# Sinkhorn steps of the stream mixer placed behind the key stages alone

## What is computed

```python
# layer 1: linear cross attention, q from layernorm(x), k and v from the context
qh = softmax(Wq q, over the 64 rows of a head) / 8
kh = softmax(Wk k, over the 2048 columns)
context = einsum('bhdn,bhen->bhde', kh, Wv v)
x = x + rmsnorm_over_channels(Wo (context applied to qh) + bo) * g * 16
# layer 2: four streams of 512 columns per token (a token is a row of 2048)
H_res = sinkhorn_log(logits_res, num_iters=50, tau=0.1)   # 4 x 4 per token
H_pre, H_post = softmax(logits_pre), softmax(logits_post)
y = einsum('btjc,btj->btc', x_streams, H_pre) @ W_branch
x = x + ((1-g) I + g H_res) mixed over the streams + y * H_post
```

## Time and profile before

| | |
|---|---|
| median of 3 runs | 2906.38 us (2905.24 to 2907.76) |
| the profiled execution | 2906.39 us, its span 2904.7 us |
| mean granted TensorE clock | 0.967 |
| TensorE busy | 2626.9 us (90%) |
| VectorE busy | 1663.3 us (57%) |
| ScalarE busy | 1033.0 us (36%) |
| GpSimd busy | 804.3 us (28%) |

### The profile page before, as it was taken

The page is one execution under the profiler, slowest core; times in us unless marked ns, Lnnn a source line. Parts: engine busy times, 40 slices in busy tenths (PEclk is TensorE's granted clock), DMA queues, the critical chain, the costliest instruction groups (busy, mean ns, idle before and its releaser), DMA issues.

```text
span 2904.7 us, 32933 instructions
## 1 busy us (share of the span) xinstructions
PE 2626.9 (90%) x11002; PEld 1735.8 (60%) x11002; DVE 1663.3 (57%) x4194; ACT 1033.0 (36%) x2312; POOL 804.3 (28%) x785
## 2 busy tenths in 40 slices
PE   7989898999989898999989999898998999999765
PEld 4766666666656566565666656566665566656411
DVE  2444434345766757355664766534587685867482
ACT  2333333334332333434333343333434333343222
POOL 1322314050422304142231513214051141512311
PEclk9999999999999999999999999999999999999878
DMA  6112121203112120413324221232413324231166
GB/s 223 37 55 91 58 95 54 92 22 107 39 55 91 59 95 29 140 61 105 120 76 128 70 89 64 82 121 67 137 61 104 122 71 133 69 100 32 52 180 169
DMA packets 203082, 258.22 MB, mean 89 GB/s; under 512 B 45218, under 2 KB 111522, under 8 KB 202914
## 3 DMA queue, kind: packets, MB, share of 16 engines
q1 hardware_dynamic: 202914, 256.12, 28.0%
HBM read 180.17 MB, written 75.89 MB: 88 GB/s over the span
## 4 chain that ended last, share of the span: by engine, by line
PE 77%; DVE 14%; ACT 3%; issue 2%; DMA 1%; POOL 1%; SPq 1%; DVEq 0%; ACTq 0%; POOLq 0%
PE big L628 16%; PE kc_bank L571 15%; PE big L546 13%; PE big L603 13%; PE tb L670 4%; PE tb L613 4%; PE tb L557 4%; PE misc L650 3%; PE tb L681 3%; DVE stats L800 2%; ACT turned L1138 2%; PE kc_bank L647 2%; DVE ska L974 1%; DVE skr L977 1%; DMA out<-mix_out 1%
## 5 line engine op out<-in xcount | busy, mean ns | idle before, releaser
L1138 ACT COPY turned<-tb 128x512 f32<-128x512 f32 x512 | 297.8, 585 | 1021.1 <-PE tb L613 692.7
L546 PE MATMUL big<-ctx_sb,wk 128*128 128x512 f32 x1024 | 515.2, 632 | 50.3 <-ACT k_exp L1129 50.1
L628 PE MATMUL big<-merged,turned 128*128 128x256 f32 x2048 | 492.9, 383 | 61.7 <-ACT turned L1138 61.1
L628 PEld LDWEIGHTS big<-merged,turned 128*128 128x128 f32 x2048 | 380.5, 190 | 206.5 <-issue 123.6
L571 PE MATMUL kc_bank<-ctxt,turned 128*128 128x256 f32 x2048 | 481.8, 379 | 6.8 <-ACT turned L1138 6.8
L603 PE MATMUL big<-wqs,x_sb 128*128 128x512 f32 x1024 | 482.0, 596 | 5.5 <-DVE q_sb L867 4.7
L1346 POOL TENSOR_TENSOR qhalf<-q_sb 128x512 f32<-128x512 f32 x128 | 162.2, 1267 | 922.4 <-ACT q_sb L1143 922.4
L571 PEld LDWEIGHTS kc_bank<-ctxt,turned 128*128 128x128 f32 x2048 | 372.3, 190 | 60.7 <-issue 20.1
L546 PEld LDWEIGHTS big<-ctx_sb,wk 128*128 128x128 f32 x1024 | 195.0, 202 | 246.2 <-issue 173.0
L773 DVE TENSOR_REDUCE kmax<-big 128x1 f32<-128x512 f32 x256 | 173.8, 686 | 286.3 <-PE big L546 285.6
L1354 POOL TENSOR_TENSOR q_sb<-q_sb,qsum 128x1024 f32<-128x1024 f32 x128 | 243.3, 1901 | 332.1 <-DVE qsum L879 332.1
(11 more groups left out here) (124 smaller groups left out, 3090.7 us busy)
## 6 DMA issues: line engine op xcount, KB each, us to landing
mix_ld<-streams SPq DMA_DIRECT2D x168, 240.0 KB
ctx_sb<-in_ctx SPq DMA_DIRECT2D x64, 512.0 KB, 9.2
ctxt<-in_ctx_t SPq DMA_DIRECT2D x64, 512.0 KB, 4.6
x_sb<-in_x SPq DMA_DIRECT2D x64, 512.0 KB, 9.0
x_tr<-in_x_t SPq DMA_DIRECT2D x64, 512.0 KB, 6.4
streams<-x_sb SPq DMA_DIRECT2D x64, 512.0 KB, 2.9
out<-mix_out SPq DMA_DIRECT2D x168, 192.0 KB, 2.2
streams<-y_sb SPq DMA_DIRECT2D x32, 256.0 KB, 2.0
```

What stands on the lines that cost most here:

```text
L546: t = nc.tensor.matmul(big[i], wk[:, ct, dt * P:(dt + 1) * P], ctx_sb[b % 2][:, ct, quarter(i)], start=ct == 0, stop=ct == CT - 1)
L628: t = nc.tensor.matmul(big[2 + p % 2][:, half], turned[n % 3][:, dt * P:(dt + 1) * P], merged[:, dt, :], start=dt == 0, stop=dt == DT - 1)
L1138: nc.scalar.copy(turned[k % 3][:], tb[n % 2][:]).then_inc(s_tba, 1)
```

## The change

```diff
     for gr in range(LAST):
-        free = [place for place in order_of_places[starts[gr]:starts[gr + 1] - 8] if place[0] != "A"]
+        free = [place for place in order_of_places[starts[gr]:starts[gr + 1] - 8] if place[0] != "Q"]
         free = free[:SINK * 8 // 7]
         for n in range(SINK):
             put(free[n * len(free) // SINK], "sink", gr)
         end = order_of_places.index(free[-1])
         put(order_of_places[end + 1], "coefs", gr)
         ready.append((end + 1, len(MIX_TILES[gr])))
```

## The result

The changed kernel takes **2940.44 us** (median, 2939.47 to 2940.66), the one before 2906.39 beside it: a ratio of 1.0115, interval 1.01 to 1.0131. That is 34 us slower, or 1.2%, in the range of 2933 to 3000, and 27 us under the forecast of 2967.

The account below looks back on a forecast made before the run. TensorE was taken as the bound nearly everywhere but the tail. Queries -30.5, keys +26 (groups of four batches) and +54 (groups of two), clock +11 made +60 on a span of 2904.7: 2967 us, range 2933 to 3000.

Parts of the forecast that it names:

- The mechanism: Key stages: length is the time of the maximum of r = 1 plus a constant, and VectorE's queue sets that time.
- The keys have room: Rival, chance 0.04: steps in A only fill VectorE's waits, keys cost under 10 us, total about 2885.
- Only the crowded groups lose: Rival, chance 0.13: VectorE catches up in batches 4 to 11, their 26 us and the clock's 11 go: 2930.
- Maximum of r = 1: Key stages: this maximum comes 5.0 us later in batch 6 and 13.7 later in batch 13.
- the clock's 1.9: Keys of batches 5, 6, 7, 9, 10, 11: new stalls lower TensorE's clock, 1.9 us each, 11 together; bounds 0 and 22.
- Keys, sum: Key stages: steps lose 26 us in groups of four batches and 54 in groups of two, plus 11 for the clock.
- second limit: Keys of batches 12 to 15: stream additions and steps in B delay VectorE's reading of the context product for TensorE's chain.
- Queries, the term that was too small: Query stretches: gain of 30.5 us as steps leave, from levels of 95.3 without mixes and 100.8 with them.
- Tail: Last group's steps in the tail: 44 mixes beside them, not 38, stay hidden; cost 0, bound 15 us.

Follow-up runs that it names:

- runs 3 and 4: Changed kernel, groups 2 and 3 as before; groups 0 and 1 use places A only in rounds 0, 1 (early A) or 2, 3: 2956.85 and 2875.92 us.
- run 5: Changed kernel, steps of groups 0 and 1 only behind the maximum of r = 1, groups 2 and 3 as before: 2855.81 us.
- run 7: Changed kernel without steps in places A of r = 0 and 1, all four groups, none in the queries: 2885.75 us.
- run 2: Changed kernel with groups 0 and 1 dealt as before, only groups 2 and 3 in the keys alone: 2945.68 us.
- Run 8: Kernel before the change, steps where they were, first mix of a group two places later: 2910.1 us.

## Why the prediction was right or wrong

**The mechanism was right**, and it is shown, not only argued: the place of a step relative to the maximum of r = 1 decides (runs 3 and 4, 81 us apart; run 5, where 29 steps behind it cost 0.3 us; run 7, 55 us below the change). "The keys have room" is half right: the room is in r = 2 and 3 and behind the maximum of r = 1, and the steps of groups 0 and 1 put there alone make the kernel 51 us faster. "Only the crowded groups lose" describes the total (run 2) but not its mechanism: batches 4 to 11 lose 25.0 us in their keys too, and their queries give 25.4 back.

**Maximum of r = 1.** Forecast for batch 6 5.0 later, measured 20.1 to 25.0. Batch 13 forecast 13.7 later than 24.4, measured 37.3, 12.9 later. Keys of batch 5 72.6 forecast, 72.2 measured; of 10 77 and 78.2; of 12 89 and 90.1; of 13 95 and 93.2; of 14 80.1 and 83.4; of 15 85.8 and 86.3. Those of batches 5 and 10 are without the clock's 1.9.

**Keys, sum.** 80 for the steps and 11 for the clock were forecast (the terms as written add up to 80.7), 81.9 measured. The sum was 9 us too high, and **the clock's cost and the second limit's did not lie where the forecast had them**. In batch 5 no clock was lost at all: 47.6 us follow the maximum before and 47.5 after, though the granted clock of the whole stage is 0.93; the low stretch lies where TensorE waits anyway. In batch 6 it was: the third context product took 2.53 us, not 1.89, the transposes 1.06, not 0.60, and 49.1 us follow the maximum. The granted clock there, in two stretches of the changed kernel:

```profile
1018.00:1020.00 2.00, 2.00 (x8) 1.59 (x7) 1.36 (x5) 2.00 (x7) 0.00 (x0) 0.58 0.00 0
1020.00:1022.00 2.00, 2.00 (x8) 1.70 (x7) 0.94 (x4) 1.62 (x7) 0.00 (x0) 0.56 0.00 0
```

Batches 9 and 10 can be told from the context products alone, L571 from the maximum to the end of the keys (batches 9, 10, 6 and 5):

```profile
core 0: us, PE busy (x) PEld busy (x), PEclk, DMA share, GB/s
1526.50:1578.40 51.90, 19.22 (x81) 14.41 (x80) 1.00 0.52 165
1701.70:1754.90 53.20, 20.33 (x80) 15.30 (x80) 0.97 0.45 149
1015.50:1064.60 49.10, 20.30 (x80) 15.25 (x80) 0.97 0.29 96
847.70:895.20 47.50, 18.99 (x80) 14.41 (x80) 1.00 0.29 100
```

Batch 10 has the low clock of batch 6, batch 9 none. So the clock cost some 1.6 us in each of batches 6 and 10 and nothing in 5, 7 (71.1, under the 73.0 forecast), 9 and 11: about 3, not 11. The term was to be one stall's price for each of six batches; it is a matter of where the fall lands. The Trainium skill's rule that waits which recur re-throttle the array ("TensorE: Matmul & The Clock Gate", "HAM oscillation — how this bites in real kernels") agrees in kind only: with the new stalls there is more low clock, but the time comes only from what lies on the path behind them.

**Queries, the term that was too small.** 30.5 was forecast and 46.2 measured, and these 15.7 are more than half of the 27 us. Without mixes the level of 95.3 came exactly (four batches, 13.9). With mixes I took the level of the earlier trace rows, 100.8, which is the stretch whose mixes stand at places 0, 4, 8, ...; at the places that the change gives them it is 99.1 with seven, or 98.3 to 98.8 with six. Run 8 shows that the mixes' places alone make this: 100.8 to 99.1 with no step moved. Batches 8 and 12 I took as batch 9 with its 101.6; they took 103.3 and 102.5 before, which would have given 1.2 more by my own level. Batch 15 gave 7.1, near its bound of 7.5, where I took 3.5: with the steps gone TensorE is busy for 88.3 of its 93.1 us.

**The second limit** came near in sum, 15.1 forecast for batches 12 to 15 and 13.6 measured behind their maxima (6.4, 2.9, 3.4 and 0.9), but in part by luck. In batches 12 and 13 it is there: the raw tile comes 10.8 us behind the maximum (10.9 forecast, 8.7 and 8.6 before), and 59.8 us follow the maximum in batch 12 (53.4 before, 5.8 forecast) and 55.9 in batch 13 (53.0 before, 4.5 forecast). TensorE waited 1.2 us for the raw tile in each of two rounds of batch 12 and 0.3 and 0.7 in batch 13, where 2 and 2.5 were forecast. In batches 14 and 15, where 2.4 were forecast for each, TensorE never waits for a raw tile. What came in its place is a cost of the clock that the forecast took as hidden in that wait: the third context product took 3.75 us, not 1.89. In batch 14, with the granted clock of a stretch within that product (0.50), and the product on the raw tile without a wait:

```profile
2429.81 3.75 PE L571 MATMUL kc_bank<-ctxt,turned 128*128 128x256 f32 x8 [4.89 <-ACT turned L1138]
...
2430.00:2432.00 2.00, 2.00 (x5) 1.63 (x6) 1.86 (x5) 2.00 (x6) 0.00 (x0) 0.50 0.00 0
...
2438.84 0.38 PE L581 MATMUL tb<-ident,chain_raw 128*128 128x128 f32 x2
```

In batch 13 the product took 3.75 us too, and there the loss and the wait for the raw tile cover the same time, as the forecast had it; how much either would cost alone no run shows.

**Tail.** 44 mixes were hidden by its steps as forecast: 175.5 us against 176.4. GpSimd and VectorE meet less: the longest L972 takes 0.44 us now and took 1.67 before, which fits the row with 1.60. How much of the 46 us in the queries comes of this, and how much of the steps being gone, no run tells apart.

## What to carry to other kernels

Ask of a free engine not how much it is idle but ahead of which instruction: here 61% busy hid a stretch of 20 us with 2.3 us of idle, and one maximum at its end set the stage. Filler work belongs behind the instruction that the bound engine waits for. There 29 steps cost 0.3 us, but 58 in a stage cost 10.7, so that room ends too; ahead of it each microsecond counts once the bound engine has used up its own 2. A level read from one stretch with fillers in it is the level of their places, so take it from the places that the change gives them.

## Unexpected of the hardware

Nearly the same granted clock costs nothing or 1.6 us, by where the low stretch falls: 0.93 over the key stage of batch 5 without loss, 0.91 in batch 6 with it. And two kernels with 51 to 52 us of VectorE's work in the stage gave 0.87 and 0.97, so the low clock goes here with longer stalls, and it adds to them: in the run with early A the product behind the stall took 3.75 us, and 49.9 us followed the maximum of batch 5, not the 47.5 of the changed kernel.
